# GpSimd adds and subtracts the two sources of each feed-forward weight piece ahead of the Hadamard products

## The reference

```python
h = _layernorm(x) * (1 + ca) + sa
x = x + ga * attention(h, weight_qkv, weight_proj)        # causal, 16 heads of 128, 4 key/value heads
h = _layernorm(x) * (1 + cb) + sb
u = fwht(h * SU_ug) / SCALE                               # transform over 256 columns
up, gate = u @ W_up.T * (Wscale_ug[:1024] * SCALE), u @ W_gate.T * (Wscale_ug[1024:] * SCALE)
v = fwht(silu(gate) * up * SU_dp) / SCALE                 # transform over 1024 columns
x = x + gb * (v @ W_down.T * (Wscale_dp * SCALE))
```

## Time and profile before

| | |
|---|---|
| median of three runs | 950.68 us |
| the profiled execution | 949.12 us |
| its span, first to last instruction | 947.2 us |
| PE busy | 924.8 us, 98% |
| PE weight loads busy | 815.1 us, 86% |
| DVE busy | 644.0 us, 68% |
| ACT busy | 504.2 us, 53% |
| POOL busy | 459.0 us, 48% |
| mean granted TensorE clock | 0.999 of full speed |

### The profile page before, as it was taken

The page is one execution under the profiler, slowest core; times in us unless marked ns, Lnnn a source line. Parts: engine busy times, 40 slices in busy tenths (PEclk is TensorE's granted clock), DMA queues, the critical chain, the costliest instruction groups (busy, mean ns, idle before and its releaser), DMA issues.

```text
span 947.2 us, 14944 instructions
## 1 busy us (share of the span) xinstructions
PE 924.8 (98%) x5536; PEld 815.1 (86%) x5536; DVE 644.0 (68%) x1312; ACT 504.2 (53%) x1062; POOL 459.0 (48%) x607
## 2 busy tenths in 40 slices
PE   5989999999999999999999999999999999999997
PEld 4878889888888898888888888888888887888886
DVE  6567667865887577647875787478757876864554
ACT  3376556654666466547664766476647665321111
POOL 2375717670767185707671767076717674120000
PEclk9999999999999999999999999999999999999999
DMA  8000100000001000000010000000001011000000
GB/s 286 23 1 1 40 1 23 1 28 1 23 2 40 1 23 1 29 1 23 1 39 1 24 1 29 1 24 1 1 1 46 1 57 45 1 14 10 22 22 22
DMA packets 10180, 21.55 MB, mean 23 GB/s; under 512 B 1281, under 2 KB 5633, under 8 KB 9985
## 3 DMA queue, kind: packets, MB, share of 16 engines
q1 hardware_dynamic: 9392, 20.45, 6.3%
q10 hardware_dynamic: 720, 0.21, 0.1%
HBM read 18.56 MB, written 2.10 MB: 22 GB/s over the span
## 4 chain that ended last, share of the span: by engine, by line
PE 79%; DVE 12%; ACT 6%; issue 2%; DMA 1%; POOL 0%; SPq 0%; DVEq 0%; ACTq 0%
PE ps L1051 18%; PE ps L1053 17%; PE ps L1052 17%; PE ps L1180 10%; PE ps L1163 5%; PE ps L1169 5%; PE ps L1166 5%; DVE ps L945 4%; ACT prob L700 3%; DVE pt_lo L949 2%; ACT pt_hi L725 2%; DVE xhat L823 1%; DVE stats L807 1%; PE ps L1075 1%; DVE vare L815 1%
## 5 line engine op out<-in xcount | busy, mean ns | idle before, releaser
L578 POOL TENSOR_TENSOR rinv<-rsum,mone 128x1 f32<-128x1 f32 x256 | 143.3, 560 | 253.9 <-ACT prob L700 253.9
L949 DVE TENSOR_TENSOR pt_lo<-ps,pt_hi 128x512 fp32r<-128x512 f32 x288 | 198.2, 689 | 61.6 <-ACT pt_hi L725 59.5
L725 ACT ACTIVATE pt_hi<-ps 128x512 fp32r<-128x512 f32 x288 | 171.0, 597 | 124.2 <-PE ps L1180 124.1
L700 ACT ACTIVATE prob<-ps,nmax 128x384 f32<-128x384 f32 (+19 forms) x256 | 184.8, 722 | 85.8 <-DVE nmax L945 84.8
L945 DVE CUSTOM_DVE_ANT_0 ps<-ps,mask_f 128x384 f32<-128x384 f32 (+19 forms) x256 | 187.6, 738 | 47.8 <-PE ps L1169 46.0
L581 POOL TENSOR_SCALAR prob<-prob,rinv 128x384 f32<-128x384 f32 (+19 forms) x256 | 191.5, 748 | 52.8 <-POOL rinv L578 52.8
L1180 PE MATMUL ps<-ident,prob 128*128 128x128 f32 x1152 | 172.0, 273 | 1.6 <-POOL prob L581 1.1
L1180 PEld LDWEIGHTS ps<-ident,prob 128*128 128x128 f32 x1152 | 140.6, 140 | 21.6 <-DVE pt_lo L949 1.9
L1051 PE MATMUL ps<-pt_hi,v_hi 128*128 128x512 f32 x288 | 134.2, 466 | 0.0
L1053 PE MATMUL ps<-pt_hi,v_lo 128*128 128x512 f32 x288 | 113.8, 395 | 0.0
L1052 PE MATMUL ps<-pt_lo,v_hi 128*128 128x512 f32 x288 | 113.4, 394 | 0.0
(11 more groups left out here) (144 smaller groups left out, 1777.1 us busy)
## 6 DMA issues: line engine op xcount, KB each, us to landing
w_raw<-in_wqkv SPq DMA_DIRECT2D x8, 640.0 KB, 4.1
wp_raw<-in_wproj SPq DMA_DIRECT2D x8, 512.0 KB, 3.4
prob<-in_wug SPq DMA_DIRECT2D x4, 512.0 KB, 4.8
out_y<-prob SPq DMA_DIRECT2D x8, 256.0 KB, 2.2
x<-in_x SPq DMA_DIRECT2D x3, 512.0 KB, 13.1
prob<-in_wmod SPq DMA_DIRECT2D x1, 1024.0 KB, 9.9
wv_raw<-in_wv SPq DMA_DIRECT2D x4, 256.0 KB, 4.5
raw_down<-in_wdn SPq DMA_DIRECT2D x1, 1024.0 KB, 4.6
```

The lines of the kernel that those rows point to most:

```text
L700: a_.activation(row(i, h).rearrange("p (a n) -> p a n", a=nb), score_banks(i, h).rearrange("p (a n) -> p a n", a=nb)[:, :, 0:w], ACT.Exp, ...
L725: a_.activation(pt_hi[:, n % 3, :], ring(t, "T", n), ACT.Copy).then_inc(pth_done, 1)
L949: v_.tensor_tensor(pt_lo[:, n % 3, :], ring(t, "T", n), pt_hi[:, n % 3, :].bitcast(F32), ALU.subtract).then_inc(ptl_done, 1)
```

## The change

Before, TensorE forms both H(a) + H(b) and H(a) - H(b) from the sources a and b of a piece: eight matmuls a piece. Now GpSimd forms a + b and a - b of the raw piece first (`last_butterfly`, two instructions of 512 columns), and TensorE multiplies each once: four matmuls a piece. The difference is written in place of b; the sum goes to a spare buffer of 512 columns. With this:

- The Hadamard matrix with the minus sign is gone, `had_r` is half as wide, and so is its transfer.
- `raw_high` and `raw_low` work on two tiles that don't lie together, so each is two instructions of 512 columns, where it was one of 1024.
- Piece 1 goes through GpSimd whole: high part (ScalarE did it before) and low part (VectorE did it before). Its two buffers are now `k_hi` and `k_lo`, the keys, which are free as soon as the last scores are done; before they were `o_hi` and `o_lo`, which are in use up to the last output projection.
- TensorE's piece 1 now waits by itself until VectorE has read the last output projection (`add_done`).
- The two stages of `butterfly` stand one window of the last turn earlier: p = 1 and 2, where they were 2 and 3.

```diff
@@ walk
-            if t + 1 == TURNS and p > 1:
-                fill[2].append((t, "B", p - 2, 0))
+            if t + 1 == TURNS and p in (1, 2):
+                fill[2].append((t, "B", p - 1, 0))
@@ buffers
-        had_r = [sb(f"had_r{n}", [P, 2 * P], F32R)[:, :] for n in range(2)]
+        had_r = [sb(f"had_r{n}", [P, P], F32R)[:, :] for n in range(2)]
...
-        raw_hi = [w_hi[:, :, 0:CH], o_hi[:, :, :]]
-        raw_lo = [w_lo[:, :, 0:CH], o_lo[:, :, :]]
+        in_keys = [a[:, :].rearrange("p (k n) -> p k n", k=KH) for a in (k_hi, k_lo)]
+        raw_hi = [w_hi[:, :, 0:CH], in_keys[0], w_hi[:, :, 0:CH], o_hi[:, :, :], w_hi[:, :, 0:CH], o_hi[:, :, :]]
+        raw_lo = [w_lo[:, :, 0:CH], in_keys[1], w_lo[:, :, 0:CH], o_lo[:, :, :], w_lo[:, :, 0:CH], o_lo[:, :, :]]
+        raw_sum = [z[:, a, :, :].rearrange("p k n -> p (k n)") for z in (sum_dn, dif_dn) for a in range(2)]
...
+        def sum_slot(piece):
+            return piece - 4 if piece > 3 else 2 + piece % 2
+        def halves_of(piece):
+            return raw_sum[sum_slot(piece)], raw[piece][:, 1, :]
@@ GpSimd
+            def last_butterfly(n):
+                a, b = raw[n][:, 0, :], raw[n][:, 1, :]
+                if n < 4:
+                    pool.wait_ge(raw_s[n], 16)
+                else:
+                    pool.wait_ge(fly_s, 2)
+                g_.tensor_tensor(raw_sum[sum_slot(n)], a, b, ALU.add)
+                g_.tensor_tensor(b, a, b, ALU.subtract).then_inc(last_fly_s, 1)
...
                 if n >= 2:
                     pool.wait_ge(fmm_s, (n - 1) * KH)
-                g_.tensor_scalar(raw_hi[n % 2], raw[PIECES[n]], 1.0, 1.0, ALU.mult, ALU.mult).then_inc(rhi_s, 1)
-            pool.wait_ge(raw_s[0], 16)
-            raw_high(0)
-            pool.wait_ge(rhi_s, 1)
-            g_.tensor_tensor(raw_lo[0], raw[0], raw_hi[0].bitcast(F32), ALU.subtract).then_inc(rlo0_s, 1)
-            pool.wait_ge(fly_s, 2)
+                if n == 3:
+                    pool.wait_ge(y_done, (TURNS + 1) * NT)
+                pool.wait_ge(last_fly_s, n + 1)
+                for k, z in enumerate(halves_of(PIECES[n])):
+                    last = g_.tensor_scalar(raw_hi[n][:, k, :], z, 1.0, 1.0, ALU.mult, ALU.mult)
+                last.then_inc(rhi_s, 1)
+            for n in range(2):
+                last_butterfly(PIECES[n])
+                if n:
+                    pool.wait_ge(s_done, this(s_done, TURNS - 1, 32))
+                raw_high(n)
+                pool.wait_ge(rhi_s, n + 1)
+                for k, z in enumerate(halves_of(PIECES[n])):
+                    last = g_.tensor_tensor(raw_lo[n][:, k, :], z, raw_hi[n][:, k, :].bitcast(F32), ALU.subtract)
+                last.then_inc(rlo01_s, 1)
             for n in range(2, len(PIECES)):
-                if PIECES[n] < 4:
-                    pool.wait_ge(raw_s[PIECES[n]], 16)
+                last_butterfly(PIECES[n])
                 raw_high(n)
@@ ScalarE
-            act.wait_ge(raw_s[1], 16)
-            act.wait_ge(y_done, (TURNS + 1) * NT)
-            a_.activation(raw_hi[1], raw[1], ACT.Copy).then_inc(rhi1_s, 1)
@@ VectorE
-                if n == 1:
-                    dve.wait_ge(rhi1_s, 1)
-                else:
-                    dve.wait_ge(rhi_s, n)
-                v_.tensor_tensor(raw_lo[n % 2], raw[PIECES[n]], raw_hi[n % 2].bitcast(F32), ALU.subtract).then_inc(rlo_s, 1)
+                dve.wait_ge(rhi_s, n + 1)
+                for k, z in enumerate(halves_of(PIECES[n])):
+                    last = v_.tensor_tensor(raw_lo[n][:, k, :], z, raw_hi[n][:, k, :].bitcast(F32), ALU.subtract)
+                last.then_inc(rlo_s, 1)
...
-            raw_low(1)
@@ TensorE
+                if n == 1:
+                    pe.wait_ge(add_done, this(add_done, TURNS - 1, NT))
+                if n < 2:
+                    pe.wait_ge(rlo01_s, n + 1)
                 else:
-                    if n > 1:
-                        pe.wait_ge(wf_ok, KH * n)
-                    pe.wait_ge(rlo_s, n)
-                mats = had_r[PIECES[n] // 4]
-                plus, minus = mats[:, 0:P], mats[:, P:2 * P]
+                    pe.wait_ge(rlo_s, n - 1)
+                    pe.wait_ge(wf_ok, KH * n)
+                mat = had_r[PIECES[n] // 4]
                 for k in range(KH):
-                    for src in (0, 1):
-                        mat = minus if k and src else plus
-                        mm(W[n][k], mat, raw_hi[n % 2][:, src, :], start=not src, stop=False)
-                        last = mm(W[n][k], mat, raw_lo[n % 2][:, src, :], start=False, stop=bool(src))
-                    last.then_inc(fmm_s, 1)
+                    mm(W[n][k], mat, raw_hi[n][:, k, :], start=True, stop=False)
+                    mm(W[n][k], mat, raw_lo[n][:, k, :], start=False, stop=True).then_inc(fmm_s, 1)
```

More of the change, by code:

```diff
@@ L241, in build @@
         guard_a, guard_b = sum_dn[:, 0, :, :], sum_dn[:, 1, :, :]
-        had_f = prob[:, 0, 0, 0:CH].rearrange("p (a n) -> p a n", a=2)
+        had_f = prob[:, 0, 0, 0:2 * P].rearrange("p (a n) -> p a n", a=2)
         raw = [prob[:, n // 2, n % 2 * 2:n % 2 * 2 + 2, CH:2 * CH] for n in range(4)]
@@ L302, in build @@
                                              sem("wf_hi"), sem("wf_ready"))
-        rlo0_s, rhi1_s = sem("raw_lo_first_done"), sem("raw_hi_second_done")
+        rlo01_s, last_fly_s = sem("raw_lo_first_done"), sem("last_butterflies")
         gu_s, silu_s, g32_s, ghi_s, g_ok = sem("gate_up_done"), sem("silu_done"), sem("g32_done"), sem("g_hi_done"), sem("g_ready")
@@ L1216, in weights @@
                     pe.wait_ge(consts, 1)
-                    pe.wait_ge(rlo0_s, 1)
-                else:
-                    if n > 1:
-                        pe.wait_ge(wf_ok, KH * n)
-                    pe.wait_ge(rlo_s, n)
-                mats = had_r[PIECES[n] // 4]
-                plus, minus = mats[:, 0:P], mats[:, P:2 * P]
-                for k in range(KH):
-                    for src in (0, 1):
-                        mat = minus if k and src else plus
-                        mm(W[n][k], mat, raw_hi[n % 2][:, src, :], start=not src, stop=False)
-                        last = mm(W[n][k], mat, raw_lo[n % 2][:, src, :], start=False, stop=bool(src))
-                    last.then_inc(fmm_s, 1)
+                if n == 1:
+                    pe.wait_ge(add_done, this(add_done, TURNS - 1, NT))
+                if n < 2:
+                    pe.wait_ge(rlo01_s, n + 1)
+                else:
+                    pe.wait_ge(rlo_s, n - 1)
+                    pe.wait_ge(wf_ok, KH * n)
+                mat = had_r[PIECES[n] // 4]
+                for k in range(KH):
+                    mm(W[n][k], mat, raw_hi[n][:, k, :], start=True, stop=False)
+                    mm(W[n][k], mat, raw_lo[n][:, k, :], start=False, stop=True).then_inc(fmm_s, 1)
             def gate_up(c, m):
@@ L1306 @@
         had = np.block([[had, had], [had, -had]])
-    had = np.concatenate([s * had / n ** 0.5 for n in (HID, INTER) for s in (1, -1)], axis=1).astype(np.float32)
+    had = np.concatenate([had / n ** 0.5 for n in (HID, INTER)], axis=1).astype(np.float32)
     arrays = {
```

## The result

The changed kernel takes 953.46 us (median of 9 runs, 951.23 to 954.95), the kernel before in the same set 950.94 (9 runs, 948.65 to 951.72): ratio 1.0027, 95% interval 1.0014 to 1.0040. The forecast was 951.0 with a range of 947.0 to 954.8 and "no change" (within 0.3%) as the likeliest. The interval leaves out 1: the changed kernel is a little slower, by 2.5 us in the median. The profiled execution took 951.54 us against 949.12 before, 2.4 us more.

A forecast was written before the change was run, and what follows sets the result against it. TensorE is 98% busy, but VectorE bounds the first chunk up to block 3's down products. Gain 0.9 and loss 2.1 give +1.2 us: 950.3 from the profiled execution, 951.9 from the median; 951.0 taken, range 947.0 to 954.8.

The forecast's parts named there:

- Part 1: Hadamard products: 24 of 48 matmuls removed, 5.5 us of TensorE's time, gained only if nothing else were late.
- Part 2: Pieces 0 and 1: ready in time, first gate product at 796.6 in place of 798.33, gain 1.7 us.
- Part 3: First chunk to 824 us: gain 3.7 us, less 2.9 for VectorE and GpSimd blocking each other, leaving 0.8 to 1.0.
- Part 4: Last turn near 749 us: earlier butterfly stage holds up VectorE's `xhat` pair, so TensorE stands 2.1 us more.
- Part 5: The rest, including the narrower matrix transfer and the `add_done` wait: worth 0 together, 0.3 us either way.
- As meant: Rival: VectorE and GpSimd hardly hinder each other, 3.7 us gained, nothing lost at 749: 945.4, 947 by the median; chance 0.12.
- the pair alone slips through: Rival: no loss at the `xhat` pair at 749, first-chunk contention stays: -0.9 us, 948.2 to 949.8; chance 0.20.
- GpSimd keeps the port over instructions: Rival: VectorE waits through successive gapless GpSimd instructions, 5 us more in the first chunk: 955.3, slower; chance 0.15.
- stall (a): Last turn, theory of the experiments: first butterfly stage beside the `xhat` pair costs 2.05 us.

The follow-up runs named there:

- twice: The changed kernel with each of its 24 Hadamard products issued twice, undoing the halving: 956.13 us, 1.0060 against the kernel before.
- clear_twice: two_stalls with each of the 24 Hadamard products issued twice: 953.36 us, 1.0033 against the kernel before.
- clear_no_sums: two_stalls without GpSimd's sums and differences of the last four pieces: 946.13 us, 0.9964 against the kernel before.
- no_sums: The changed kernel without GpSimd's sums and differences of the last four pieces, raw halves multiplied instead: 951.75 us, 1.0023 against the kernel before.
- write_only: As no_sums, but GpSimd clears two unneeded buffers in place of each sum and difference left out: 950.87 us, 1.000 against the kernel before.
- stages_only: The kernel before with only the two butterfly stages moved one window earlier: 951.5 us, 1.0022 against the kernel before.
- stage0_late: The changed kernel with the first butterfly stage four score blocks later in the same window, past the `xhat` pair: 949.98 us, 1.0008 against the kernel before.
- had_act: The changed kernel with the Hadamard matrices rounded by ScalarE instead of VectorE: 952.16 us, 1.0030 against the kernel before.
- two_stalls: The changed kernel with both the edits of stage0_late and had_act: 948.59 us, 0.9980 against the kernel before.
- high_act: two_stalls with the high parts of the last four pieces written by ScalarE instead of GpSimd: 947.16 us, 0.9967 against the kernel before.

## Why the prediction was right

The forecast of no change was right, narrowly: the ratio of 1.0027 lies just inside the 0.3% that it calls no change, the interval (to 1.0040) reaches beyond, and the time is 2.5 us above the 951.0 named. Each mechanism it names is there. Sizes, by its own steps:

- **Part 1** (5.5 us of products). Busy time of PE fell by 5.5. They are worth 2.5 to 3.05 us (twice, clear_twice).
- **Part 2** (gain 1.7 up to the first gate product). Relative to P0, G0 came 1.69 us earlier. Right. Piece 1 was ready at 795.0, as for the late landing considered (GpSimd began at 782.06), and still hidden.
- **Part 3** (3.7 without contention, 2.9 for contention, 0.8 to 1.0 left at D3). Measured: 3.06 without the sums of the last four pieces (clear_no_sums), 30.12 - 27.24 = 2.9 for the sums (after against no_sums), 0.18 left. The mechanism was right, and the price of contention came out by luck: of the seven places four were held up, six instructions by 0.75 us each in the mean where the sum had 0.42 for a place, 4.5 us in all, and 1.2 of that lay in time in which VectorE would else have waited for ScalarE (0.19 of idle time ahead of the gated product of block 0, where it is 1.39 in clear_no_sums). Nor is the price a constant: with both stalls gone it is 29.53 - 27.24 = 2.3. The mis-sized term is the first: waits for ScalarE's Silu taken as "two or three near 0.3", 1.0 us in sum, are 1.39 at block 0 and 0.23 at block 2 once the sums are gone. That the two-input subtraction is held up, which no row of before showed, is now shown (1.66 for 0.69). The Trainium skill (SBUF — State Buffer, "Who interferes with whom") has it so, and says too that a GpSimd instruction that only writes leaves such a subtraction alone; the trace of write_only agrees (1.28 for the pair).
- **Part 4** (pair 2.1 us longer, TensorE 2.1 more). 3.11 for 1.05, idle 2.22 for 0.17, +2.05 at P0. Right, and shown from both sides by stages_only and stage0_late. What the prediction left out is the clock, which fell behind this stall in the profiled executions of stages_only and twice and cost another 1.5 us there. The margin of the last score block held: no wait for GpSimd in the last row.
- **Part 5** ("worth 0 together"). Here is the step that failed. It counted what the narrower matrix saved and put the rounding of that matrix beside GpSimd's low part of piece 0 at nothing, though both kernels have the two side by side. 1.52 for 0.49, 0.72 us of TensorE (had_act's trace: 0.71 back; two_stalls: P0 back at 45.14). Why the pair was not held up before is open. That it met GpSimd unhindered in one trace said nothing about the changed list, where starts and gaps differ by tenths of a us.

Sum: +2.05 + 0.72 - 0.18 = +2.6 against the forecast's +1.2; the profiled executions differ by 2.4. Of the shortfall about half is part 5 and half part 3.

The rivals fell. "As meant" needed unhindered durations; "the pair alone slips through" needed 1.05 for the pair; "GpSimd keeps the port over instructions" needed VectorE to stand behind sum and difference together. In the first chunk the longest hold-up of one instruction is 1.07 us, less than one GpSimd sum (1.28), and at the pair the second `xhat` ended 0.15 us behind the sum though the difference followed without a gap (751.38): one instruction was waited for each time.

**Left open.** Why had_act gives no gain in time with stall (a) still in place. The drop of the clock behind (a) would explain it if it came more often there. Two of the six kernels with (a) show it in their profiled execution, and none of the six without. On the chip where had_act ran, 14 of the 25 executions of the three kernels with (a) had a mean clock of 0.997 or less, 1 of 11 of stage0_late, and 6 of 25 of the kernel before. That makes it likely and doesn't show it, for the mean clock doesn't say where in the kernel it fell.

## What to carry to other kernels

Work given to GpSimd is not free while VectorE's instructions read and write only ordinary on-chip memory: each side waits for the running instruction of the other. Give a part of it to ScalarE, which no GpSimd instruction held up here (high_act), or put it beside work of VectorE that reads TensorE's result buffer; the second is suggested by unhindered rows such as the one at 803.10 and was not tried. And when a stream is inserted, walk down the other engines' lists at the new times: about half of what was lost here (2.05 and 0.72 us) was lost not in the chunk that the change is about (2.9), but in the last turn ahead of it. Halving an engine's work is worth what the next engine's chain leaves: 3 us of 5.5.

## What was not expected of the hardware

TensorE's clock is granted at half after some stands and not after others. Two kernels that are alike at this place, early in the first turn, clear_twice and then clear_no_sums (columns as above, the last two the share and GB/s of transfers):

```profile
52.00:54.00 2.00, 1.10 (x7) 1.10 (x8) 0.60 (x1) 1.88 (x4) 1.63 (x3) 0.87 0.01 4
...
56.00:58.00 2.00, 1.92 (x6) 1.79 (x6) 0.69 (x1) 1.10 (x5) 1.59 (x5) 0.50 0.00 0
```

```profile
52.00:54.00 2.00, 1.17 (x9) 1.17 (x10) 0.67 (x2) 1.81 (x4) 1.70 (x3) 1.00 0.01 4
...
56.00:58.00 2.00, 1.86 (x12) 1.82 (x13) 1.15 (x2) 0.94 (x5) 1.59 (x5) 1.00 0.00 0
```

In both TensorE was busy for about 1.1 us from 52 to 54. In the first it then ran at 1.2 GHz for six to seven us and came to the last turn's `xhat` pair at 750.36 in place of 748.37: 2 us. Five of the twelve profiled executions have such a drop near 54 us (no_sums, write_only, two_stalls, twice, clear_twice), and none of these edits touches that place. In two_stalls and twice it lasted about 3.4 us, by the granted clock of their windows, and their pairs came at 748.27 and 748.56, not late.

The kernel before has slower executions too: of its 61 in the three sets of experiments, 19 had a mean clock of 0.997 or less and a median of 951.18 us, 32 had 0.999 or 1.000 and a median of 949.46. Set by set the two medians are 951.26 and 949.37, 951.65 and 949.04, but 951.11 and 950.74 in the set of two_stalls: there even the executions at full clock were slow, so the clock is not the whole of it, and the rest stays open. These differences are up to 0.2%, as much as most edits here, so a ratio of medians moves with how many such executions fall on either side. Marks counted from one instruction of the trace leave out what was lost ahead of it. What decides whether the clock falls was not tried.
